# A fused attention and expert kernel: the weighted sum over values as 64x64 native products, the null value subtracted on VectorE, and the norm statistics of the input taken in groups

## Chip, cores and metric

The kernel runs on one core of a Trainium2 chip, as one program. The metric is device microseconds from start to end of an execution.

## What is computed

The input x is 32 sequences of 64 tokens with 256 features. A layer norm, a causal attention of 16 heads that share one key and one value head, a decayed retrieval, a two-of-eight expert layer and a dense layer follow. The change touches the attention, of which this is the core (`nk` and `nv` are a null key and a null value):

```python
xn = ln(x, g_norm)
q = (xn @ Wq).reshape(b, n, HEADS, DIM_HEAD).transpose(0, 2, 1, 3)
kv = xn @ Wkv
k, v = (kv[..., :DIM_HEAD], kv[..., DIM_HEAD:])
k = jnp.concatenate([nk, k], axis=1)
v = jnp.concatenate([nv, v], axis=1)
...
attn = jax.nn.softmax(sim + attn_bias, axis=-1)
out = jnp.einsum('bhij,bjd->bhid', attn, v)
return ln(out @ Wout, g_out)
```

Since the weights of a row sum to 1, the kernel computes the sum over v - nv without the null column and adds nv afterwards.

## The kernel before

**Tiles and steps.** Two sequences make a tile of 128 rows, so there are 16 tiles. Every engine runs a hand-written `body(i, par, live, part)` for i = -2 to 18; `live(off)` says whether tile i + off exists. So in one step an engine works on up to five tiles: tile i + 1 is projected, tile i scored, tile i - 1 weighted and summed, tile i - 2 projected out, tile i - 3 put through the retrieval. Steps -2 to 3 and 14 to 18 are written out, with one-off work between them (`at_step`, and the functions given to `pipeline`); steps 4 to 13 are a loop. There is no scheduler: each engine executes in the order written and waits on semaphores.

**TensorE, step i.** Output projection of tile i - 2 from the upper and lower halves of oT (16 products, lines 322 and 323, then 8, line 1339); transposes of kn2 (1344), of qn (1351, two groups of four), of xn of tile i + 1 (1357); two products of the retrieval (1363, 1369), of which the second waits for qT; scores (1375): 32 products of 64x64 by 65 columns in native float32; 1388; transposes of the weights pr (1400); the qkv projection of tile i + 1 (317 to 319) into banks 3, 2, 1, three split passes for each half of the 256 features, with the null product (1417) at the end of bank 3; transposes of zn (1407); the weighted sum (AV); 317 to 319 for the retrieval's output; 1443.

**Split and native.** Most matrices are held as two float32r halves (`_h`, `_l`), and `split_passes` multiplies three times. For AV, `vblk` is a 128x128 block matrix that carries the value tile twice on its diagonal, in an upper half (copied by ScalarE, 713, four 64x64 pieces) and a lower half (subtracted by VectorE, 986, four pieces). The weights are transposed into PSUM and split too (ScalarE 683, VectorE 1015). AV is then two sequences by three passes of 512 columns. The null value reaches bank 3 by a product of two rows, `ones` by `nvhl` (1417).

**Norms.** For tile i + 2 VectorE takes bn_stats and bn_aggr (974, 978) between the two parts of the q and k norm sums (1020, 1023), and GpSimd makes scale and bias in four small operations (564 to 570), ahead of `mask_bias` (524). ScalarE then makes xn (660).

**VectorE's order, steady step:** vblk_l, statistics of the output norm (974, 978), xnT_l (993), at (998), sim (1004, three), mx (1007), rT_l (1011), pT_l (1015), ss and sc, statistics of x, ss and sc twice, oT_l (1038, two), den (1041), rden (1044), xs (1047), qn (1055, three). **GpSimd's:** pr (542), which needs rden; output norm (545 to 551); every second step the half of an expert's weights (528); sim less its maximum (556); rn (561, three); norm of x; biasm (524). After step -1 GpSimd copies the null key into kh (496), for which TensorE waits before step 0. After the last tile GpSimd scatters the rows to the experts (579), 32 indirect transfers one after the other.

## Time and profile before

| | us |
|---|---|
| timed runs (3) | 531.86, 532.69, 539.52 |
| median | 532.69 |
| profiled execution, span from first to last instruction | 532.0 |
| PE busy | 468.7 (88%) |
| DVE busy | 359.7 (68%) |
| ACT busy | 274.7 (52%) |
| POOL busy | 284.7 (54%) |

The profile gives no other time of the profiled execution than its span, so times of the trace are set against 532.0. PE is TensorE's matmuls, DVE VectorE, ACT ScalarE, POOL GpSimd. A matmul's record is longer than the time until the next can start, since matmuls are pipelined; where they follow without a wait, the distance between starts is the cost. A native float32 product has two records, a split pass and a transpose one.

### The profile page before, as it was taken

What the parts mean: (1) busy time and instruction counts of PE and PEld (TensorE: products, weight loads), DVE (VectorE), ACT (ScalarE), POOL (GpSimd) and SP (SyncE); (2) the same over time, 40 slices, a digit from 0 to 9 for tenths busy, and PEclk for the clock granted to TensorE, in tenths of its full rate; (3) what the DMA queues carried; (4) which work ended last, traced back from release to release, by engine and by line L of the source; (5) the groups of instructions that cost most, each with busy time, mean ns of one, the idle gap of its engine ahead of it and who ended that gap; (6) DMA issues with size and microseconds to landing.
All of it is one profiled execution on the core that took longest, in us unless ns stands there. A gap on an engine that the chain in (4) does not pass through costs nothing.

```text
span 532.0 us, 11898 instructions
## 1 busy us (share of the span) xinstructions
PE 468.7 (88%) x3961; PEld 418.7 (79%) x3961; DVE 359.7 (68%) x879; ACT 274.7 (52%) x574; POOL 284.7 (54%) x343
## 2 busy tenths in 40 slices
PE   3946889999999999999999896499989489999997
PEld 1735777898999988898888785398989359898986
DVE  4784888888889888898766475757664524444522
ACT  3426666576667666566652422246565234453442
POOL 3738778897987979797830777400000633425100
PEclk9966999999999999999998998989999879999999
DMA  8370103709082641000010323265752312213011
GB/s 263 90 192 1 31 1 111 257 26 343 0 292 72 208 157 30 0 30 1 1 31 2 99 100 108 82 206 185 235 169 100 89 33 57 80 41 96 25 41 39
DMA packets 51616, 52.17 MB, mean 98 GB/s; under 512 B 6645, under 2 KB 49015, under 8 KB 51577
## 3 DMA queue, kind: packets, MB, share of 16 engines
q1 hardware_dynamic: 47956, 42.98, 25.5%
q0 software_dynamic: 3072, 8.39, 5.0%
q8 instruction: 23, 0.38, 0.3%
q10 hardware_dynamic: 548, 0.28, 0.2%
q14 instruction: 17, 0.13, 0.1%
HBM read 22.03 MB, written 29.62 MB: 97 GB/s over the span
## 4 chain that ended last, share of the span: by engine, by line
PE 59%; issue 8%; POOL 8%; ACT 5%; DMA 3%; DVE 3%; SPq 1%; DVEq 0%; ACTq 0%; POOLq 0%
PE bank L317 10%; PE bank L318 9%; PE bank L319 9%; POOL slot_x L579 6%; PE bank L322 5%; PE bank L323 5%; PE bank L1375 3%; PE bank L1655 3%; PE bank L1400 2%; PE bank L1339 2%; PE bank L1443 2%; ACT qT L666 2%; PE bank L1351 1%; PE bank L1388 1%; DMA slot_y<-yb 1%
## 5 line engine op out<-in xcount | busy, mean ns | idle before, releaser
L588 POOL DMA_INDIRECT yg<-slot_y,yrow x32 | 34.2, 1068 | 120.8 <-DMA slot_y<-yb 76.3
L561 POOL TENSOR_TENSOR rn<-sc,half 128x6 f32<-128x6 f32 (+1 forms) x48 | 60.6, 1277 | 7.9 <-DVE sc L1023 6.9
L1256 DVE TENSOR_TENSOR hl<-hw,hh 128x512 fp32r<-128x512 f32 x32 | 22.2, 693 | 57.1 <-ACT hw L837 57.1
L835 ACT ACTIVATE hh<-bank,late 128x512 fp32r<-128x512 f32 x32 | 22.0, 688 | 53.5 <-PE bank L1655 41.9
L317 PE MATMUL bank<-wqkv_h,xnT_h 128*128 128x384 f32 x96 | 39.1, 408 | 6.8 <-DVE sim L1004 6.8
L556 POOL TENSOR_TENSOR sim<-sim,mx 128x1040 f32<-128x1040 f32 x16 | 31.3, 1955 | 23.0 <-DVE mx L1007 23.0
L695 ACT ACTIVATE sq<-bank 128x384 f32<-128x384 f32 (+1 forms) x48 | 22.8, 475 | 40.3 <-PE bank L319 24.7
L524 POOL TENSOR_TENSOR biasm<-bias,mneg 128x1040 f32<-128x1040 f32 x16 | 35.7, 2229 | 3.7 <-DMA bias<-rel_scratch 3.7
L579 POOL DMA_INDIRECT slot_x<-xs,posi x32 | 31.4, 980 | 11.2 <-issue 9.4
L542 POOL TENSOR_TENSOR pr<-pe,rden 128x1024 f32<-128x1024 f32 x16 | 30.4, 1903 | 9.2 <-DVE rden L1044 4.5
L322 PE MATMUL bank<-wout_h,oT_h 128*128 128x256 f32 x128 | 33.6, 296 | 1.9 <-DVE oT_l L1038 1.9
L318 PE MATMUL bank<-wqkv_l,xnT_h 128*128 128x384 f32 x96 | 34.5, 359 | 0.0
L319 PE MATMUL bank<-wqkv_h,xnT_l 128*128 128x384 f32 x96 | 34.3, 358 | 0.0
L322 PE MATMUL bank<-w_h,hh 128*128 128x256 f32 x128 | 32.5, 287 | 0.0
L323 PE MATMUL bank<-wout_l,oT_h 128*128 128x256 f32 x128 | 32.4, 289 | 0.0
L323 PE MATMUL bank<-w_l,hh 128*128 128x256 f32 x128 | 32.0, 283 | 0.0
L1020 DVE TENSOR_REDUCE ss<-sq 128x6 f32<-128x384 f32 (+1 forms) x48 | 25.2, 526 | 7.5 <-ACT sq L695 7.4
L1004 DVE TENSOR_TENSOR sim<-bank,biasm 128x455 f32<-128x455 f32 (+1 forms) x48 | 21.9, 513 | 11.2 <-PE bank L1375 11.2
L674 ACT ACTIVATE zn<-bank,nb,rs 128x256 f32<-128x256 f32 x16 | 9.1, 566 | 39.4 <-POOL nb L551 39.4
L317 PE MATMUL bank<-wu_h,bxT_h 128*128 x80 | 25.1, 314 | 2.5 <-DVE bxT_l L1205 2.5
L322 PEld LDWEIGHTS bank<-wout_h,oT_h 128*128 128x128 f32 x128 | 24.9, 195 | 2.5 <-issue 1.4
L317 PEld LDWEIGHTS bank<-wqkv_h,xnT_h 128*128 128x128 f32 x96 | 19.5, 204 | 9.1 <-issue 8.3
(317 smaller groups left out, 1604.8 us busy)
## 6 DMA issues: line engine op xcount, KB each, us to landing
slot_x<-zrow SPq DMA_DIRECT2D x4, 4352.0 KB, 14.4
xq<-slot_x SPq DMA_DIRECT2D x40, 128.0 KB, 2.1
slot_y<-yb SPq DMA_DIRECT2D x20, 256.0 KB, 2.4
fstage<-in_f_W SPq DMA_DIRECT2D x4, 512.0 KB, 4.5
out<-p_all SPq DMA_DIRECT2D x8, 256.0 KB, 2.1
xs<-in_x SPq DMA_DIRECT2D x1, 1536.0 KB, 9.5
raw_out<-in_c_Wout SPq DMA_DIRECT2D x1, 1024.0 KB, 7.8
stage<-in_m_wgate SPq DMA_DIRECT2D x8, 128.0 KB, 2.1
```

Source lines behind the costliest of these rows:

```text
L317: e.matmul(dst, stat[0], mov[0], start=start, stop=False, **kw)
L318: e.matmul(dst, stat[0], mov[1], start=False, stop=False, **kw)
L319: return e.matmul(dst, stat[1], mov[0], start=False, stop=stop, **kw)
L322: e.matmul(dst, stationary, moving[0], start=start, stop=False, **kw)
L323: e.matmul(dst, stationary, moving[1], start=False, stop=False, **kw)
L524: e.tensor_tensor(biasm[:, :, :], bias[:, :, :], (mneg[:, i:i + 1, :] if isinstance(i, int) else mneg[:, bass.ds(i, 1), :]).to_broadcast([ ...
L542: e.tensor_tensor(pr[:, :].rearrange('p (h k) -> p h k', h=H), pe[:, :, 0:S], rden[:, :].rearrange('p (h o) -> p h o', o=1).to_broadcast([ ...
L556: e.tensor_tensor(sim[:, :, :], sim[:, :, :], mx[:, :].rearrange('p (h o) -> p h o', o=1).to_broadcast([P, H, NK]), ALU.subtract).then_inc ...
L561: e.tensor_tensor(rn[:, lo:hi], sc[:, lo:hi], half[:, lo:hi], ALU.pow).then_inc(sems['rn'], 1)
L579: e.indirect_dma_start(out=xdram.ap()[:, :], out_offset=bass.IndirectOffsetOnAxis(ap=posi[:, t, r:r + 1], axis=0), in_=xs[:, t, :], in_off ...
L588: e.indirect_dma_start(out=yg[:, g % 2, r, t, :], out_offset=None, in_=ydram.ap()[:, :], in_offset=bass.IndirectOffsetOnAxis(ap=yrow[:, g ...
L1020: e.reduce_sum(ss[:, lo:hi], sq[:, lo:hi, :], AX_X).then_inc(sems['ss'], 1)
```

## The change

- **AV.** `split_passes` with `vblk` and the halves of pT is replaced by four native float32 products of 64x64 by 512 columns, one for each quarter of the array. For that the head parity of the second sequence is swapped: rows r of qT meet sequence b at r ^ b, in scores and AV, and the biases and null biases are loaded in the same order (three transfers for the bias, not two; two for `nulls`, not one). pT is one float32 copy; pT_l, vblk_h, vblk_l and their zeroing go.
- **Null value.** The product 1417 goes. VectorE makes v_own and v_other (three operations of 64 columns) from bank 3 less `nvB`, at the end of its step.
- **Norm of x.** Statistics of x are taken for groups of tiles, 1, 1, 2, 4, 4 and 4 of them: `row_stats(n)` on VectorE at the start of step -2 and at the very end of steps -1 to 3, `norm_rows(n)` on GpSimd after the same steps. The loop has none of it.
- **Order.** ScalarE makes kn2 before oT_h and exp, not after. VectorE makes qn before xs, den and rden. TensorE's eight lower passes of the output projection come after the transposes of qn, and the waits of AV stand before the last bank of qkv.

```diff
+        X_GROUPS = ((0, 1), (1, 2), (2, 4), (4, 8), (8, 12), (12, NT))
+
+        def x_groups_for(i):
+            return [n for n, (lo, hi) in enumerate(X_GROUPS) if lo <= i < hi][0] + 1 if isinstance(i, int) else len(X_GROUPS)
...
+            def norm_rows(n):
+                t0, t1 = X_GROUPS[n]
+                e.wait_ge(sems['mvx'], 2 * (n + 1))
+                e.tensor_tensor(nmx[:, t0:t1], mvx[:, t0:t1, 0], fixed[:, 1:2].to_broadcast([P, t1 - t0]), ALU.mult)
+                e.tensor_tensor(vex[:, t0:t1], mvx[:, t0:t1, 1], fixed[:, 0:1].to_broadcast([P, t1 - t0]), ALU.add).then_inc(sems['ln1_ve'], 1)
+                e.wait_ge(sems['ln1_ve'], n + 1)
+                e.tensor_tensor(rsx[:, t0:t1], vex[:, t0:t1], half[:, 0:t1 - t0], ALU.pow).then_inc(sems['ln1_rs'], 1)
+                e.wait_ge(sems['ln1_rs'], n + 1)
+                e.tensor_tensor(nbx[:, t0:t1], nmx[:, t0:t1], rsx[:, t0:t1], ALU.mult).then_inc(sems['ln1_nb'], 1)
...
                 e.wait_ge(sems['rn'], NB3)
-                e.wait_ge(sems['ln1_nb'], 2)
+                norm_rows(1)
                 e.wait_ge(sems['v_null'], 2)
                 e.tensor_copy(kh[:, :, S], colsc[:, NKK:NKK + 1].to_broadcast([P, 2])).then_inc(sems['p_tables'], 1)
...
             def after_first_scores():
+                norm_rows(2)
...
             def mask_decay():
+                norm_rows(4)
...
             def after_second_scores():
+                norm_rows(3)
...
-                    e.wait_ge(sems['ln1_nb'], due(i + 2 if live(1) else NT))
...
-                    e.wait_ge(sems['mv1'], due(2 * (i + 3)))
...
-                    e.tensor_tensor(nb1[:, :], nm1[:, :], rs1[:, :], ALU.mult).then_inc(sems['ln1_nb'], 1)
...
+            pipeline(e, body, {-2: after_norm0, -1: after_first_projection, 0: after_first_scores, 1: after_second_scores, 2: mask_decay, 3: lambda: norm_rows(5)})
...
+                    e.wait_ge(sems['ln1_nb'], x_groups_for(i + 1 if isinstance(i, int) else i))
...
+                    e.activation(xn[:, :], at_tile(xs, i + 1), ACT.Identity, bias=at_col(nbx, i + 1), scale=at_col(rsx, i + 1)).then_inc(sems['xn'], 1)
...
+                        e.activation(pT[:, 4 * c:4 * c + 4, :], bank[4 + c][:, :].rearrange('p (b t) -> p b t', b=4), ACT.Copy).then_inc(sems['pT'], 1)
...
+                if live(1):
+                    e.wait_ge(sems['rn'], due(NB3 * (i + 1) + 1))
+                    e.wait_ge(sems['kT_t'], due(i + 1))
+                    e.activation(kn2[:, :, :], bank[NB3][:, QB - 2 * DH:QB - DH].rearrange('p (o d) -> p o d', o=1).to_broadcast([P, 2, DH]), ACT.Copy, scale=rn[:, H:H + 1]).then_inc(sems['kn2'], 1)
...
-                if live(1):
-                    e.wait_ge(sems['av_t'], due(2 * i))
-                    e.wait_ge(sems['qkv'], due(NB3 * (i + 2)))
-                    for b, r in ((0, 0), (0, 1), (1, 0), (1, 1)):
-                        last = e.activation(vblk_h[r * DH:(r + 1) * DH, 1 - par, b, r * DH:(r + 1) * DH], bank[NB3][b * S:(b + 1) * S, QB - DH:QB], ACT.Copy)
-                    last.then_inc(sems['v_h'], 1)
-                    e.wait_ge(sems['rn'], due(NB3 * (i + 1) + 1))
-                    e.wait_ge(sems['kT_t'], due(i + 1))
-                    e.activation(kn2[:, :, :], bank[NB3][:, QB - 2 * DH:QB - DH].rearrange('p (o d) -> p o d', o=1).to_broadcast([P, 2, DH]), ACT.Copy, scale=rn[:, H:H + 1]).then_inc(sems['kn2'], 1)
...
+            def row_stats(n):
+                t0, t1 = X_GROUPS[n]
+                e.wait_ge(sems[('ld_x0', 'ld_x0', 'ld_x1', 'ld_x2', 'ld_x2', 'ld_x2')[n]], 16 * 1)
+                for t in range(t0, t1):
+                    last = e.bn_stats(stx[:, t - t0, :], xs[:, t, :])
+                last.then_inc(sems['mvx'], 1)
+                e.wait_ge(sems['mvx'], 2 * n + 1)
                 settle(e)
-                e.bn_aggr(mv[:, n, :], st6[:, n, :]).then_inc(sems[m], 1)
+                for t in range(t0, t1):
+                    last = e.bn_aggr(mvx[:, t, :], stx[:, t - t0, :])
+                last.then_inc(sems['mvx'], 1)
+                e.wait_ge(sems['mvx'], 2 * n + 2)
 
...
+                if isinstance(i, int) and i == FIRST_I:
+                    row_stats(0)
...
-                if live(0):
...
-                        last = e.tensor_tensor(vblk_l[at_b], bank[NB3][b * S:(b + 1) * S, QB - DH:QB], vblk_h[at_b].bitcast(F32), ALU.subtract)
...
-                if live(-1):
-                    for c in range(2):
-                        e.wait_ge(sems['pT_h'], due(2 * (i - 1) + c + 1))
-                        e.tensor_tensor(pT_l[:, 4 * c:4 * c + 4, :], bank[4 + c][:, :].rearrange('p (b t) -> p b t', b=4), pT_h[:, 4 * c:4 * c + 4, :].bitcast(F32), ALU.subtract).then_inc(sems['pT_l'], 1)
...
-                if live(2):
-                    if isinstance(i, int):
-                        e.wait_ge(sems['ld_x0' if i + 2 < 2 else 'ld_x1' if i + 2 < 4 else 'ld_x2'], 16 * 1)
-                    layer_norm_stats(at_tile(xs, i + 2), 0, i + 2, 'mv1', 'ln1_nb')
...
-                if live(0):
-                    e.wait_ge(sems['pe'], due(i + 1))
-                    e.reduce_sum(den[:, :], pe[:, :, :], AX_X).then_inc(sems['den'], 1)
-                    e.wait_ge(sems['den'], due(i + 1))
-                    e.wait_ge(sems['pr'], due(i))
-                    e.reciprocal(rden[:, :], den[:, :]).then_inc(sems['rden'], 1)
-                if live(-3):
-                    e.wait_ge(sems['vo_t'], due(i - 2))
-                    e.tensor_tensor(at_tile(xs, i - 3), bank[4][:, 0:D], at_tile(xs, i - 3), ALU.add).then_inc(sems['x1'], 1)
...
+                if live(-3):
+                    e.wait_ge(sems['vo_t'], due(i - 2))
+                    e.tensor_tensor(at_tile(xs, i - 3), bank[4][:, 0:D], at_tile(xs, i - 3), ALU.add).then_inc(sems['x1'], 1)
+                if live(0):
+                    e.wait_ge(sems['pe'], due(i + 1))
+                    e.reduce_sum(den[:, :], pe[:, :, :], AX_X).then_inc(sems['den'], 1)
+                    e.wait_ge(sems['den'], due(i + 1))
+                    e.wait_ge(sems['pr'], due(i))
+                    e.reciprocal(rden[:, :], den[:, :]).then_inc(sems['rden'], 1)
+                if live(1):
+                    e.wait_ge(sems['av_t'], due(2 * i))
+                    if isinstance(i, int) and i == -1:
+                        e.wait_ge(sems['v_nv'], 1)
+                    values = slice(QB - DH, QB)
+                    e.tensor_tensor(v_own[:, 1 - par, :], bank[NB3][:, values], nvB[:, :], ALU.subtract)
+                    for b in range(2):
+                        other = slice((1 - b) * S, (2 - b) * S)
+                        last = e.tensor_tensor(v_other[other, 1 - par, :], bank[NB3][b * S:(b + 1) * S, values], nvB[b * S:(b + 1) * S, :], ALU.subtract)
+                    last.then_inc(sems['v'], 1)
+                if isinstance(i, int) and FIRST_I < i < FIRST_I + len(X_GROUPS):
+                    row_stats(i - FIRST_I)
...
                     for c in range(HP):
                         upper_passes(e, bank[6][:, 0:D], (wout_h[:, c, :], wout_l[:, c, :]), oT_h[:, c, :], c == 0)
-                    e.wait_ge(sems['oT_l'], due(2 * (i - 1)))
-                    for c in range(HP):
-                        last = e.matmul(bank[6][:, 0:D], oT_l[:, c, :], wout_h[:, c, :], start=False, stop=c == HP - 1)
...
-                    e.wait_ge(sems['x1'], due(i - 3))
...
+                if live(-2):
+                    e.wait_ge(sems['oT_l'], due(2 * (i - 1)))
+                    for c in range(HP):
+                        last = e.matmul(bank[6][:, 0:D], oT_l[:, c, :], wout_h[:, c, :], start=False, stop=c == HP - 1)
+                    last.then_inc(sems['wo_t'], 1)
...
+                    e.wait_ge(sems['v'], due(i + 1))
...
-                    head = slice(r * DH, (r + 1) * DH)
                     for b in range(2):
+                        head = slice((r ^ b) * DH, ((r ^ b) + 1) * DH)
                         last = e.matmul(dst[b * S:(b + 1) * S, lo:lo + NK], qT[head, c, b * S:(b + 1) * S], kh[head, b, :], start=True, stop=True)
...
+                def before_av():
+                    e.wait_ge(sems['pT'], due(2 * i))
+                    e.wait_ge(sems['v'], due(i))
+                    e.wait_ge(sems['zn'], due(i - 1))
+                    e.wait_ge(sems['rT_l'], due(i - 2))
...
+                        if m == NB3 - 1 and live(-1):
+                            before_av()
...
-                        if c == NB3 - 1:
-                            last = e.matmul(bank[NB3][:, QB - DH:QB], ones[0:2, :], nvhl[:, :], start=False, stop=True, skip_group_check=True)
...
-                    e.wait_ge(sems['pT_l'], due(2 * i))
-                    e.wait_ge(sems['vblk'], due(i))
-                    e.wait_ge(sems['zn'], due(i - 1))
-                    e.wait_ge(sems['rT_l'], due(i - 2))
-                    for b in range(2):
-                        last = split_passes(e, bank[6 + b][:, :], (vblk_h[:, 1 - par, b, :], vblk_l[:, 1 - par, b, :]), (pT_h[:, :, b * S:(b + 1) * S], pT_l[:, :, b * S:(b + 1) * S]), True, True)
-                        last.then_inc(sems['av_t'], 1)
+                    if not live(1):
+                        before_av()
+                    for q in range(2):
+                        rows = slice(q * S, (q + 1) * S)
+                        for b in range(2):
+                            r = q ^ b
+                            value = (v_other if r else v_own)[rows, 1 - par, :]
+                            last = e.matmul(bank[6 + b][r * DH:(r + 1) * DH, :], value, pT[rows, :, b * S:(b + 1) * S], start=True, stop=True)
+                            if q == 1:
+                                last.then_inc(sems['av_t'], 1)
```

What VectorE does between the norm of q of one step and the scores of the next, steps 1 and 2 of the kernel before:

```order
L1038 SCALAR_TENSOR_TENSOR oT_l<-bank,colsc,oT_h 128x8x64 x2
L1041 TENSOR_REDUCE den<-pe 128x16
L1044 RECIPROCAL rden<-den 128x16
L1055 TENSOR_TENSOR qn<-bank,rn 128x256
L1055 TENSOR_TENSOR qn<-bank,rn 128x384 x2
L986 TENSOR_TENSOR vblk_l<-bank,vblk_h 64x64 x4
L974 BN_STATS st<-bank 128x6
L254 MEMSET carrier 128x1
L978 BN_AGGR mv<-st 128x2
L993 TENSOR_TENSOR xnT_l<-bank,xnT_h 128x256
```

and the same place now, with the statistics of tiles 4 to 7 (stx, mvx) in it:

```order
L1030 SCALAR_TENSOR_TENSOR oT_l<-bank,colsc,oT_h 128x8x64 x2
L1038 TENSOR_TENSOR qn<-bank,rn 128x256
L1038 TENSOR_TENSOR qn<-bank,rn 128x384 x2
L1044 TENSOR_REDUCE den<-pe 128x16
L1047 RECIPROCAL rden<-den 128x16
L1053 TENSOR_TENSOR v_own<-bank,nvB 128x64
L1056 TENSOR_TENSOR v_other<-bank,nvB 64x64 x2
L972 BN_STATS stx<-xs 128x6 x4
L253 MEMSET carrier 128x1
L977 BN_AGGR mvx<-stx 128x2 x4
L987 BN_STATS st<-bank 128x6
```

The three qn moved ahead of den and rden, and four bn_stats and four bn_aggr stand between the value pieces and the next step's work.

GpSimd, after step 1, before:

```order
L561 TENSOR_TENSOR rn<-sc,half 128x6 x2
L564 TENSOR_TENSOR nm<-mv,fixed 128x1
L565 TENSOR_TENSOR ve<-mv,fixed 128x1
L568 TENSOR_TENSOR rs<-ve,half 128x1
L570 TENSOR_TENSOR nb<-nm,rs 128x1
L524 TENSOR_TENSOR biasm<-bias,mneg 128x1040
L542 TENSOR_TENSOR pr<-pe,rden 128x1024
```

and now:

```order
L581 TENSOR_TENSOR rn<-sc,half 128x6 x2
L545 TENSOR_TENSOR biasm<-bias,mneg 128x1040
L494 TENSOR_TENSOR nmx<-mvx,fixed 128x4
L495 TENSOR_TENSOR vex<-mvx,fixed 128x4
L497 TENSOR_TENSOR rsx<-vex,half 128x4
L499 TENSOR_TENSOR nbx<-nmx,rsx 128x4
L562 TENSOR_TENSOR pr<-pe,rden 128x1024
```

The norm of x moved from ahead of biasm to between biasm and pr, and it waits for the statistics that VectorE makes last in the step.

## Rows read from the trace of the kernel before

**Rows 1.** Busy time by stretch: window, its length, busy us and count of each engine, clock.
```profile
105.21:254.33 149.12, 146.29 (x1561) 134.19 (x1561) 131.59 (x328) 98.80 (x225) 127.93 (x146) 1.00 0.31 103
```

**Rows 2.** Timeline of PE, one steady step: start, us, line, operands, count, idle before.
```profile
149.91 0.39 PE L317 MATMUL bank<-pT_h,vblk_h 128*128 128x512 f32 x1
...
151.30 0.28 PE L317 MATMUL bank<-wvo_h,rT_h 128*128 128x256 f32 x1
...
152.03 1.06 PE L1443 MATMUL bank<-znT,mqk 128*128 128x128 f32 x8
...
157.68 0.49 PE L1369 MATMUL bank<-uT,znT 128*128 128x128 f32 x2 [0.27 <-ACT qT L666]
158.10 1.15 PE L1375 MATMUL bank<-kh,qT 64*64 64x65 f32 x60
159.18 0.71 PE L1388 MATMUL bank<-at,zn 128*128 128x128 f32 x4
...
161.90 0.33 PE L319 MATMUL bank<-wqkv_h,xnT_l 128*128 128x384 f32 x1
162.16 0.29 PE L1417 MATMUL bank<-nvhl,ones 2*128 2x64 f32 x1
...
162.66 0.34 PE L318 MATMUL bank<-wqkv_l,xnT_h 128*128 128x384 f32 x1
```

**Rows 3.** Timeline of DVE, the same step.
```profile
151.59 1.41 DVE L1038 SCALAR_TENSOR_TENSOR oT_l<-bank,colsc,oT_h 128x512 fp32r<-128x512 f32 x2 [0.20 <-ACT oT_h L704]
...
154.91 1.34 DVE L1055 TENSOR_TENSOR qn<-bank,rn 128x256 f32<-128x256 f32 x3
156.17 0.91 DVE L986 TENSOR_TENSOR vblk_l<-bank,vblk_h 64x64 fp32r<-64x64 f32 x4
```

**Rows 4.** Groups by line and form, 105.21 to 254.33: busy us, mean ns.
```profile
L568 POOL TENSOR_TENSOR rs<-ve,half 128x1 f32<-128x1 f32 x10 | 5.5, 548 | 0.8
...
L974 DVE BATCH_NORM_STATS2 st<-xs 128x6 f32 x9 | 3.8, 427 | 0.0
...
L978 DVE BATCH_NORM_AGGREGATE mv<-st 128x2 f32<-128x6 f32 x19 | 3.4, 180 | 0.5
```

**Rows 5.** Timeline of PE, start of the kernel.
```profile
27.91 0.33 PE L1344 MATMUL bank<-ident,kn 128*128 128x128 f32 x1 [1.28 <-POOL kh L496]
...
37.71 0.66 PE L317 MATMUL bank<-wqkv_h,xnT_h 128*128 128x384 f32 x1 [5.76 <-DVE sim L1004]
...
55.64 0.42 PE L317 MATMUL bank<-wqkv_h,xnT_h 128*128 128x384 f32 x1 [0.54 <-DVE sim L1004]
```

**Rows 6.** The page's clock row: granted TensorE clock in 40 slices, tenths of full speed.
```profile
PEclk9966999999999999999998998989999879999999
```

**Rows 7.** Timeline of DVE, step 2.
```profile
62.55 1.24 DVE L1041 TENSOR_REDUCE den<-pe 128x16 f32<-128x1040 f32 x1 [0.18 <-ACT pe L708]
```

**Rows 8.** Timeline of POOL, step 2.
```profile
66.40 1.90 POOL L542 TENSOR_TENSOR pr<-pe,rden 128x1024 f32<-128x1024 f32 x1 [0.31 <-issue]
```

**Rows 9.** Timeline of PE, AV and the transposes of pr, steps 2 to 4.
```profile
59.28 0.39 PE L317 MATMUL bank<-pT_h,vblk_h 128*128 128x512 f32 x1
...
68.36 1.09 PE L1400 MATMUL bank<-ident,pr 128*128 128x128 f32 x8
...
73.81 0.39 PE L317 MATMUL bank<-pT_h,vblk_h 128*128 128x512 f32 x1
...
85.59 1.09 PE L1400 MATMUL bank<-ident,pr 128*128 128x128 f32 x8
...
90.33 0.39 PE L317 MATMUL bank<-pT_h,vblk_h 128*128 128x512 f32 x1
...
100.48 1.09 PE L1400 MATMUL bank<-ident,pr 128*128 128x128 f32 x8
```

**Rows 10.** Timeline of PE, AV after the last projection.
```profile
268.05 0.50 PE L317 MATMUL bank<-pT_h,vblk_h 128*128 128x512 f32 x1 [0.24 <-DVE pT_l L1015]
```

**Rows 11.** Timeline of POOL, the first scatter to the experts.
```profile
296.15 1.25 POOL L579 DMA_INDIRECT slot_x<-xs,posi  x1 [1.71 <-DVE posi L1118]
```

More of the change, by code:

```diff
@@ L131, in adaln_attention_ffn @@
             kh = s1('kh', [P, 2, NK])
-            vblk_h = s1('vblk_h', [P, 2, 2, P], F32R)
-            vblk_l = s1('vblk_l', [P, 2, 2, P], F32R)
+            v_own = s1('v_own', [P, 2, DH])
+            v_other = s1('v_other', [P, 2, DH])
             sim = s1('sim', [P, H, NK])
@@ L233, in adaln_attention_ffn @@
                     t_hT t_mlp t_fold    unit_h unit
-                    mv1 ln1_ve ln1_rs ln1_nb xn xnT xnT_h xnT_l qkv sq ss ss_c rn qn kn2 v_h
-                    kT_t kh sc7 vblk qT_t qT sim_t biasm sim mx simc pe den rden pr
-                    pT_t pT_h pT_l av_t oT_h oT_l wo_t mv2 ln2_ve ln2_rs ln2_nb zn
+                    mvx ln1_ve ln1_rs ln1_nb xn xnT xnT_h xnT_l qkv sq ss ss_c rn qn kn2 v
+                    kT_t kh sc7 qT_t qT sim_t biasm sim mx simc pe den rden pr
+                    pT_t pT av_t oT_h oT_l wo_t mv2 ln2_ve ln2_rs ln2_nb zn
                     znT_t znT uT_t uT sc_t at rt_t rT_h rT_l vo_t x1
```

93 lines of the change are left out of this document (34 added, 59 removed).

## The prediction

> **What bounds the kernel now.** I read first the busy time by stretch. From the AV of step 4 to that of step 14, 105.21 to 254.33, PE is busy for 146.29 of 149.12 us at a granted clock of 1.00 [rows 1]. That is ten steps of 14.91 us and PE bound. DVE is next with 131.59 of 149.12, so a shorter PE step soon meets DVE. Then I read the timelines of one such step on PE and DVE, for distances between starts [rows 2, 3]. What is saved there reaches the end one for one, because the 32 scatters that follow the pipeline start only when the router's positions are there [rows 11], and nothing behind them is touched. Last I read steps -1 to 4. There PE is no bound: it waits for kh, sim and pr [rows 5, 9], and the change puts work on exactly these chains. So the sum has two halves, a steady gain and a cost at the edge.
>
> **The steady step.** *AV.* Six split passes take 151.30 - 149.91 = 1.39 us, 0.23 each [rows 2]. Now it is four native products of 512 columns, eight records. Eight native records of 128 columns take about 1 us (L1443, 1.06 with the last one's tail), so 128 columns cost some 0.12 and 512 some 0.45. Whether the quarters work at once decides: 60 score records of 64x65 take 159.18 - 158.10 = 1.08 us, 18 ns each, although one lasts far longer, so there four quarters do run abreast [rows 2]. I take two passes, all quarters abreast, 0.9, and 0.3 for entering and leaving the 64x64 form: 1.2, a gain of 0.2. Bounds are 0.9 and 3.6 (all eight in turn).
>
> *Null product.* From 161.90 to 162.66 two starts lie 0.76 apart where two passes of 384 columns would take 0.34 (0.17 each, three quarters of the 0.23 of 512); L1417 costs 0.42, and it goes [rows 2].
>
> *qT wait.* L1369 waits 0.27 for qT, and its records end in 158.10 - 157.68 = 0.42 where four of 0.12 stand for two products [rows 2]; the eight lower passes, some 1 us (256 columns each, 0.12), now stand between the transposes of qn and this product. I take 0.45 of stall and 0.1 of refill off, -0.5, if DVE gives qn no later. DVE's qn starts at 154.91, 5.0 behind AV [rows 3]; with den, rden and xs behind it, it starts at 3.4. The v pieces are new: three of 64 columns, at the 0.23 of one of the four vblk_l (0.91) [rows 3], 0.7 against 0.91. pT_l, vblk_l and bn_stats with bn_aggr of x (0.43 and 0.18) leave DVE [rows 4]; with pT_l of 1024 columns at the rate of oT_l (1.41 for as many, rows 3) and the lighter v its load falls by some 2.1 us a step. ACT loses four small copies, GpSimd 1.2 us (one power of 0.55 and three small operations, rows 4). In the other direction, AV and kn2 wait for work later on ACT's and GpSimd's orders every second step, about 0.1.
>
> Sum: -0.2 - 0.4 - 0.5 + 0.1 = -1.0 us a step, bounds -0.7 and -1.1, so 13.9 instead of 14.9. Over ten steps -10.
>
> **The edges.** Here each item delays a chain on which PE waits.
>
> (a) Step -1. kT_0 at 27.91 waited 1.28 for kh on GpSimd [rows 5]. `norm_rows(1)` (1.3 us) needs `row_stats(1)`, which DVE now takes after qn (three, 1.3) and v (0.7), where it stood ahead of the second sums. I work it out as +2.6, plus 0.3 for the further transfer of nulls: +2.9 on 27.91, and so on 37.71. Bounds +1.5 and +3.5.
>
> (b) Step 0, QKV of tile 1. The null product goes, -0.45 at that clock. The clock row shows 0.6 in two slices of 13.3 us, 26.6 to 53.2 [rows 6]; if it comes back at the same moment as before, a part of the 6 us of passes runs at 2.4 and not at 1.2 GHz: -1.2 (0 to -1.7). xn of tile 2 in step 1 then waits for the group of tiles 2 and 3, whose statistics follow rden and v, and for GpSimd's norm behind biasm: +2.5. Altogether QKV of tile 2 (55.64 [rows 5]) at +3.7, and less its null product +3.3.
>
> (c) Step 2. Now DVE's den starts at 62.55 [rows 7]. With qn ahead (1.3) it starts at 63.7, rden ends at 65.2, v at 65.9. Four bn_stats at 0.43 and four bn_aggr at 0.18 [rows 4] with a settle make 2.6: 68.5. GpSimd has been waiting in `norm_rows(3)`; its four operations, of four columns, take 1.3 to 1.7: 70.1. Behind them stands pr, which started at 66.40 and lasts 1.90 [rows 8]: ends 72.1. PE's transposes of pr stood at 68.36, 9.1 behind AV [rows 9]; they slip by 3.7. QKV of tile 3 stood 0.5 later than it had to, by sim, so 3.2 of it remain, less 0.4 of the null product: +2.8.
>
> (d) Step 3, the same group size with the decay mask in front. The transposes stood at 85.59, 11.8 behind AV [rows 9], so much of it was there already; I work out pr's end at 13.4 behind AV: +1.25 net.
>
> (e) Step 4. The transposes stood at 100.48, 10.2 behind AV [rows 9]. GpSimd has the weight split in this step and is late by 0.7; pr's end comes at 14.0: +3.5 net.
>
> Sum of the edges: 3.3 + 2.8 + 1.25 + 3.5 = +10.9, bounds +7 and +14 (they differ by the settle and waits between engines that these chains take seven times, and by the clock).
>
> **The tail.** Step 15 saves the qT wait (0.5), AV 14 stood at 268.05 waiting 0.24 for pT_l, which is gone [rows 10], and steps 14 to 15 save AV: -1.5. The scatters, 296.15 on, each some 1.25 us [rows 11], are as before.
>
> Total: -10 + 10.9 - 1.5 = -0.6 on the span of 532.0, 531.4. The median of the runs shown lies 0.7 above this span, so 532.0 in its terms. Two of a hundred, which is about what a measurement tells from no change, are 522.0 and 543.3.
>
> **Rivals.**
>
> 1. *The edges are cheap.* The grouped statistics hide behind waits that I have put on the path, above all in step -1 and step 4, or PE catches up in steps 5 and 6, since DVE and GpSimd now have slack there. For it: PE's waits for sim (5.76 at 37.71, [rows 5]) show slack of other engines in steps 0 and 1. Against it: at 68.36 the transposes start within 0.1 of pr's end [rows 8, 9], so there a delay goes straight to PE. Half of the edge cost gone is 526, the lowest bound (+4, and the steady step at -1.1) some 521. Range 519 to 526.
>
> 2. *The clock falls.* In steps 2 to 4 PE would stand still for up to 4 us at a time, and the granted clock was low at the start, in a stretch where PE waited 5.76 us [rows 5, 6]. If it falls once, I take 5 us of columns at half the clock, less what the waits hide: +4, so 536.
>
> 3. *The quarters do not run abreast where two row halves write to one bank; slower.* Before, the row halves of the scores wrote different banks (bank 2 - r) at all but the last pair, so the 18 ns a record say nothing of one bank. Now both row halves of AV write bank 6 + b, and by r ^ b those of the scores one bank too, with other partitions. If they take turns there, AV has four passes of 0.45 in place of two, +0.9 a step over 16 steps: +14, 546. With the scores, whose 1.08 would then be 2.0, it is 560. It decides from +0.7 a step, where ten steps give 2%. For it, that nothing in this trace shows the overlap on one bank; against it, that the last pair (bank 3, both halves) does so within 60 records at no visible cost.
>
> The Trainium skill says in TensorEngine Tiling (Array Packing), "Gotcha 1: PSUM Pressure", that different row tiles cannot access the same PSUM bank simultaneously. By that rule the third rival would be the outcome, 546 to 560; no stretch of this trace shows it for long operands, and the last pair speaks against it for short ones.
>
> 4. *All eight records in turn*, 3.6 for AV: +35, 567. The 18 ns speak against it.
>
> **How the numbers follow.** Forecast 0.56 (526 to 538 as its own range); cheap edges 0.24; clock 0.10; one bank 0.08; in turn 0.02. The likeliest gives 532.0. The range goes from 522.5, within the first rival, to 543, past the second; left out are about 0.11 below and 0.10 above. Faster by over 2%: half of the first rival, 0.12. Slower: the last two, 0.10. Within 2%: 0.78.
>
> **What would show it.** Steady distance between AVs 13.9; AV itself 1.2, with eight records, and vo right behind; L1369's wait gone. kT_0 at about 30.8. In steps 2, 3 and 4 PE waits some 3.5, 1.5 and 3.5 us at the transposes of pr, released by GpSimd, and GpSimd's wait ahead of it ends on mvx of DVE. Scatters begin at 295.5. It is wrong in the edges if PE's wait in step 4 is under 2 us; wrong in AV if the eight records take over 1.6; wrong in the steady step if PE waits at oT_l or at `at` for 0.3 or more.

## The result, and the profile after

| | before | changed |
|---|---|---|
| timed runs | 531.46, 531.86, 532.69, 539.52 | 535.91, 536.45, 541.78, 544.53 |
| median, us | 532.28 | 539.12 |
| span of the profiled execution | 532.0 | 534.1 |

The ratio is 1.0103, 95% interval 1.0058 to 1.0147: 1% slower, within 2%, and inside the range of 522.5 to 543. The two executions over 1.5% above the fastest of their kernel, 539.52 and 544.53, count in the medians but not in the ratio. The forecast was 532.0 and no change, so it missed by a loss that is clear of noise. The profiled execution of the changed kernel is its fastest, 535.91. It is 2.1 us longer than the one before, and this is what the traces account for; the rest of the median's 6.8 us these two traces do not show; I come to it under e8 and e12.

The page of the changed kernel:

```profile
span 534.1 us, 11692 instructions
...
PE 464.9 (87%) x3977; PEld 408.3 (76%) x3977; DVE 337.3 (63%) x816; ACT 261.3 (49%) x510; POOL 275.4 (52%) x302
...
PEclk9956889979999999999998998979999969999999
```

Every engine has less to do, DVE by 22 us. The clock row has about what [rows 6] had at the third and fourth slice (5 and 6, where it was 6 and 6), and new falls at the fifth, sixth and ninth (53 to 80 and 107 to 120 us).

Busy time by stretch, the same view as [rows 1]; the last column but two is the granted clock. First the stretch without PE work in step 2 and the 4 us behind it, then a stretch behind a shorter wait in step 3, then the wait of step 4 and the 4 us behind it, last the ten steady steps:

```profile
69.30:73.20 3.90, 0.00 (x0) 0.00 (x0) 3.79 (x12) 0.00 (x0) 3.47 (x6) 1.00 0.02 4
73.20:77.20 4.00, 3.94 (x17) 3.94 (x18) 0.56 (x4) 1.91 (x4) 2.92 (x6) 0.57 0.00 0
90.40:94.40 4.00, 3.58 (x18) 3.20 (x19) 2.86 (x5) 0.82 (x3) 3.79 (x6) 0.57 0.00 0
104.50:109.50 5.00, 0.01 (x1) 0.02 (x1) 2.47 (x13) 0.99 (x3) 2.53 (x5) 0.84 1.04 346
109.50:113.50 4.00, 3.99 (x68) 3.56 (x69) 1.25 (x3) 1.74 (x4) 1.98 (x5) 0.50 0.40 134
119.05:258.62 139.57, 139.57 (x1571) 124.09 (x1570) 116.19 (x271) 90.77 (x185) 117.09 (x106) 1.00 0.33 110
```

Ten steps take 139.57 in place of 149.12, 13.96 each. Timeline of PE in one of them, answering to [rows 2]:

```profile
160.97 0.64 PE L1441 MATMUL bank<-pT,v_own 64*64 64x512 f32 x1
160.98 0.65 PE L1441 MATMUL bank<-pT,v_other 64*64 64x512 f32 x2
160.99 1.05 PE L1441 MATMUL bank<-pT,v_own 64*64 64x512 f32 x2
161.46 0.60 PE L1441 MATMUL bank<-pT,v_other 64*64 64x512 f32 x2
161.47 0.59 PE L1441 MATMUL bank<-pT,v_own 64*64 64x512 f32 x1
161.99 0.39 PE L323 MATMUL bank<-wvo_h,rT_h 128*128 128x256 f32 x1
...
168.12 0.48 PE L1373 MATMUL bank<-uT,znT 128*128 128x128 f32 x2
168.53 1.15 PE L1379 MATMUL bank<-kh,qT 64*64 64x65 f32 x60
169.61 0.71 PE L1392 MATMUL bank<-at,zn 128*128 128x128 f32 x4
```

The eight records of AV start in two groups, 0.01 us apart within a group and 0.49 from one group to the next: four quarters work at once, with both row halves on one bank. AV takes 161.99 - 160.97 = 1.02 us (1.39 before). The scores, now with both row halves on one bank too, still take 1.08. L1373 waits for nothing.

The edge, PE's timeline with its waits (from kT of step 0 to the AV of step 4), answering to [rows 5] and [rows 9]:

```profile
29.55 0.48 PE L1342 MATMUL bank<-ident,kn 128*128 128x128 f32 x1 [3.62 <-POOL kh L514]
...
38.61 0.66 PE L323 MATMUL bank<-wqkv_h,xnT_h 128*128 128x384 f32 x1 [4.09 <-DVE sim L1005]
...
60.80 0.64 PE L1441 MATMUL bank<-pT,v_own 64*64 64x512 f32 x1
...
73.26 1.55 PE L1404 MATMUL bank<-ident,pr 128*128 128x128 f32 x8 [4.01 <-POOL pr L562]
...
79.26 0.64 PE L1441 MATMUL bank<-pT,v_own 64*64 64x512 f32 x1
...
90.79 1.17 PE L1392 MATMUL bank<-at,zn 128*128 128x128 f32 x4 [1.60 <-DVE at L999]
...
97.68 0.64 PE L1441 MATMUL bank<-pT,v_own 64*64 64x512 f32 x1
...
109.51 0.66 PE L1361 MATMUL bank<-ident,xn 128*128 128x128 f32 x2 [4.99 <-ACT kh L673]
...
119.05 0.64 PE L1441 MATMUL bank<-pT,v_own 64*64 64x512 f32 x1
```

The AV of steps 1 to 4, which is that of tiles 0 to 3, begins at 60.80, 79.26, 97.68 and 119.05, in place of 59.28, 73.81, 90.33 [rows 9] and 105.21 [rows 1]; the distances are the prediction's steps 2, 3 and 4. (The expectations below call the last of them the AV of step 3, after its tile.) The loss is 1.5 before the first of these, then 3.9, 1.9 and 6.5, together 13.8 us (13.84). The steady steps give 9.55 of it back, the last two steps 1.15, the way from there to the end 1.0: +2.1.

### The profile page after: what moved, and what is told of

The parts are those of the page before. It is cut to its first block, busy times and chain, and to the rows that moved or that the text cites. A ratio compares the mean times of both kernels' runs of the same rounds, so it can differ in the third digit from the quotient of the medians.

```text
span 534.1 us, 11692 instructions
## 1 busy us (share of the span) xinstructions
PE 464.9 (87%) x3977; PEld 408.3 (76%) x3977; DVE 337.3 (63%) x816; ACT 261.3 (49%) x510; POOL 275.4 (52%) x302
## 4 chain that ended last, share of the span: by engine, by line
PE 64%; POOL 10%; issue 9%; DVE 8%; ACT 4%; DMA 3%; SPq 1%; DVEq 0%; ACTq 0%; POOLq 0%
PE bank L323 9%; PE bank L324 8%; PE bank L325 8%; POOL slot_x L590 6%; PE bank L328 5%; PE bank L329 5%; PE bank L1379 4%; PE bank L1404 3%; PE bank L1667 3%; PE bank L1441 3%; PE bank L1350 2%; PE bank L1355 2%; PE bank L1455 2%; PE bank L1392 2%; POOL yg L599 1%
## 5 line engine op out<-in xcount | busy, mean ns | idle before, releaser
L1260 DVE TENSOR_TENSOR hl<-hw,hh 128x512 fp32r<-128x512 f32 x32 | 22.2, 693 | 57.8 <-ACT hw L842 57.8
L705 ACT ACTIVATE sq<-bank 128x384 f32<-128x384 f32 (+1 forms) x48 | 22.8, 475 | 30.8 <-PE bank L325 30.4
L1030 DVE SCALAR_TENSOR_TENSOR oT_l<-bank,colsc,oT_h 128x512 fp32r<-128x512 f32 x32 | 22.5, 746 | 12.4 <-ACT oT_h L718 12.4
```

## Experiments

Each ran with a profile and, beside it, the kernel before on the same chip. The kernel before took 547.0 beside e1 to e4, 532.6 beside e5 to e8, and 546.7 beside e9 to e12, so only ratios compare the totals of different groups; inside a trace I use the step length, the AV starts, and the first scatter, which ends the part that the change touches.

### e1 and e11: the statistics per tile again

```diff
-                if isinstance(i, int) and FIRST_I < i < FIRST_I + len(X_GROUPS):
-                    row_stats(i - FIRST_I)
...
                     sums(0)
+                if live(2):
...
+                    layer_norm_stats(at_tile(xs, i + 2), 0, i + 2, 'mv1', 'ln1_nb')
```

(and GpSimd's four operations of one column back ahead of biasm.)

> The changed kernel with one part undone: the statistics of x and the norm's scale and bias are made per tile again, in their old places on VectorE (between the two parts of the sums) and GpSimd (ahead of biasm); AV, null value and order stay new. Theory 1 (the 13.8 us lost up to the AV of step 3 are the grouped statistics, standing in front of pr, xn and at): the AV of step 3 comes at 104 to 107 us in place of 119.05, no wait of PE for pr or xn in steps 2 and 4, the granted clock stays full after 60 us, the step stays at 13.96, and the time is 519 to 523. Theory 2 (it is the new order, with qn ahead of den and kn2 ahead of exp, that makes pr late, and the group adds little): the AV of step 3 stays behind 112 and the time over 528. Rival within theory 1: 0.6 us more on VectorE and 1.2 on GpSimd a step make the steady step 14.3, then 524 to 526.

Measured: ratio 0.9758 (0.9716 to 0.9800). Run again in another group (e11):

> e1_ungroup once more, beside e9_best and e12_before on one chip: the steps 13.94 and 14.36 again, the first scatter 13 to 15 us before that of e12_before. In e1_ungroup the way from the first scatter to the end was 248.9 us, against 235.8 in the profile of the kernel before, taken on another chip; if that belongs to the chip or the execution and not to the kernel, here it is the same as in e12_before within 1 us, or the runs of one kernel spread by 5 to 10 us.

Ratio 0.9765 (0.9735 to 0.9795). In e1 the transposes of pr in step 4 start at 95.8, in place of 100.5 before and 114.6 in the changed kernel, and the AV behind them at 100.2, earlier than either theory had it. The clock does not fall there, and the steady step is 14.17, not 13.96, so that the rival within theory 1 (14.3) was nearer; here the two stretches of the edge and the steady steps:

```profile
57.00:85.00 28.00, 23.43 (x279) 20.59 (x276) 23.77 (x54) 19.65 (x39) 24.42 (x30) 1.00 0.04 10
85.00:113.00 28.00, 27.51 (x314) 24.26 (x312) 23.65 (x62) 17.04 (x37) 24.44 (x30) 1.00 0.51 167
95.82:237.47 141.65, 140.12 (x1575) 123.82 (x1571) 120.22 (x301) 87.83 (x185) 127.89 (x146) 1.00 0.35 115
```

So theory 1 holds: without the grouping the rest of the change is 2.4% faster than the kernel before, and this version beats both. The AV of step 4 comes 18.8 us earlier than in the changed kernel (17.6 in e11, at 101.4), more than the 13.8 of the loss: without the grouping the rest of the change shortens the edge too, by 1.5 us beside the kernel before on the same chip (e12, 102.9). e11's first scatter, at 285.0, comes 8.9 before that of e12 at 293.9, not 13 to 15: the expectation had set e1 against a trace of another chip. e1 pays 0.2 us a step in the steady state: 13.9 and 14.4 by turns, the latter where GpSimd also splits an expert's weights, so that rn, and behind it kn2, oT_h and oT_l, come late. That is what the grouping had bought in the ten steady steps, 2 us.

### e2: the grouping alone

```diff
+                if isinstance(i, int) and FIRST_I < i < FIRST_I + len(X_GROUPS):
+                    row_stats(i - FIRST_I)
...
+            pipeline(e, body, {-2: after_norm0, -1: after_first_projection, 0: after_first_scores, 1: after_second_scores, 2: mask_decay, 3: lambda: norm_rows(5)})
```

> The kernel before with only the grouping of the statistics put in (VectorE takes them after qn at the end of steps -1 to 3, GpSimd at its new places); products, value blocks and order are the old ones. Theory 1: the steady step stays 14.9 (PE bound), the edge costs 9 to 14 us, so 541 to 546. Theory 2: the grouping alone costs under 5 us, so under 538.

Ratio 1.0288 (1.0245 to 1.0331), +15.7 us on a kernel before of 547; the steady step stays 14.91. pr's transposes of step 4 start at 113.5 in place of 100.5, and the AV behind them at 118.3 in place of 105.2, 13 us later. Theory 1 again, from the other side.

### e3 and e7: the order without the products, the products without the order

e3 is e1 with the old order:

```diff
-                if live(-2):
-                    e.wait_ge(sems['oT_l'], due(2 * (i - 1)))
-                    for c in range(HP):
-                        last = e.matmul(bank[6][:, 0:D], oT_l[:, c, :], wout_h[:, c, :], start=False, stop=c == HP - 1)
-                    last.then_inc(sems['wo_t'], 1)
...
```

(these lines back ahead of the transpose of kn2, kn2 behind exp on ScalarE, den, rden and xs ahead of qn on VectorE.)

> As e1_ungroup, and the order is the old one too: kn2 after exp, den, rden and xs before qn, the lower passes of the output projection before the transposes. What stays of the change is the native AV on values less the null value and the dropped null product. From distances in the trace (AV 1.39 to 1.02, the last bank 0.3 less, 0.1 for entering AV, the qT wait back) the step should be 14.3 to 14.4, and the time 524 to 527. If the order gives nothing it equals e1_ungroup within 1 us; if the order is what costs at the edge it is faster than e1_ungroup.

Ratio 0.9911 (0.9879 to 0.9942). The step is 14.78, not 14.3 to 14.4: a miss. With the old order PE's transposes of qn start 0.42 behind that of kn2 where they start 0.11 behind it in the changed kernel (and in the kernel before, where PE came later), and the wait for qT is there again:

```profile
167.24 0.27 PE L1335 MATMUL bank<-ident,kn 128*128 128x128 f32 x1
167.66 1.12 PE L1343 MATMUL bank<-ident,qn 128*128 128x128 f32 x8
...
169.49 0.49 PE L1361 MATMUL bank<-uT,znT 128*128 128x128 f32 x2 [0.27 <-ACT qT L670]
```

So PE's shorter products are mostly eaten by waits on the chain through kn2, qn and qT; products and null value alone are worth 0.13 us a step.

e7 is the other half, the kernel before with PE's lower passes moved and qn ahead of xs, den and rden, kn2 left where it was:

```diff
+                        if c == 0:
+                            e.wait_ge(sems['x1'], due(i - 3))
...
+                if live(-2):
+                    e.wait_ge(sems['oT_l'], due(2 * (i - 1)))
```

> The kernel before with a part of the new order alone: PE's lower passes of the output projection behind the transposes of qn, and on VectorE qn ahead of xs, den and rden; kn2 stays where it was on ScalarE, behind exp and the value blocks, products, value blocks and statistics are the old ones. If the wait for qT (0.44) is an item of its own, the step falls from 14.91 to 14.4 to 14.5 and the time by 7 to 8 us (ratio 0.986). If the order pays only with the shorter products and the lighter ScalarE, since qn still waits for kn2, the step stays over 14.7 (ratio 0.994 or more).

Ratio 1.0264 (1.0231 to 1.0298). The step is 16.0: over 14.7, as the second theory had it, but neither theory had foreseen a loss. VectorE stands before qn, and PE before its second product of the retrieval; timeline of both in one step:

```profile
157.56 1.35 DVE L1046 TENSOR_TENSOR qn<-bank,rn 128x256 f32<-128x256 f32 x3 [1.36 <-ACT kn L717]
...
162.12 0.48 PE L1371 MATMUL bank<-uT,znT 128*128 128x128 f32 x2 [0.70 <-DVE vblk_l L986]
```

kn2 is still behind exp and the four copies of vblk_h on ScalarE, so qn, now first on VectorE, holds up den, rden and vblk_l behind it. So this part of the order costs by itself. Whether the old products with kn2 first as well would gain was not tried.

### e4: PE kept busy where it stood still

```diff
+                if isinstance(i, int) and i == 2:
+                    for _ in range(32):
+                        e.transpose(bank[4][:, 0:P], ident[:, :], ident[:, :])
```

(and 12 of them in step 3 ahead of the wait for at; the results are overwritten, so these products only keep PE at work.)

> The changed kernel with 32 idle transposes of the identity on PE in step 2 ahead of the transposes of pr (where PE stood still for 4.0 us) and 12 in step 3 ahead of the second product of the retrieval (1.6 us). They take about 3.5 and 1.3 us and shift nothing if they end in the wait. Theory A (the granted clock falls to half because PE stood still there): the clock is 1.00 between 73 and 77 us and at 91, where it was half, and up to 2 us are gained before step 4; the fall after the 5 us stall of step 4 stays. Theory B (the clock falls whatever PE does there): the same dips, and the time is the same or 1 us more.

Busy time by stretch, behind the filled wait of step 2, and at the wait of step 4, which wasn't filled:

```profile
72.00:76.00 4.00, 3.83 (x26) 3.79 (x27) 1.33 (x7) 2.44 (x6) 3.03 (x6) 1.00 0.00 0
...
105.00:110.00 5.00, 3.17 (x62) 2.89 (x64) 0.72 (x2) 2.73 (x6) 3.41 (x7) 0.52 0.69 235
```

Theory A: the clock stays full in steps 2 and 3, and falls in step 4 as before. From the transposes of pr in step 2 to those in step 3 it is 17.57 us in place of 19.15 (92.41 - 73.26); 1.6 us of that distance were the clock. Against e8, a second execution of the changed kernel in which the distance is 20.24, it is 2.7. Ratio 1.0027 (1.0005 to 1.0050); the changed kernel wasn't run on that chip.

### e6: ScalarE's wait in the loop

```diff
-            return [n for n, (lo, hi) in enumerate(X_GROUPS) if lo <= i < hi][0] + 1 if isinstance(i, int) else len(X_GROUPS)
+            return [n for n, (lo, hi) in enumerate(X_GROUPS) if lo <= i < hi][0] + 1 if isinstance(i, int) else 4
```

> The changed kernel with one number changed: in the loop ScalarE waits for four groups of norms (tiles 0 to 7) ahead of xn, not for all six, so that in step 4 it no longer waits for the norm of tiles 12 to 15, which GpSimd makes at the very end of the edge. [...] Theory of the trace of the changed kernel (only xn's wait and the clock after it): the same wait gone and hardly a wait left, step 4 under 16, over 5 us faster.

The rival to this is the prediction's own theory: in step 4 it is pr that comes late, behind the norm of the last group, and that wait stays when xn's is gone. With the edit the loop no longer waits for the last two groups at all, so the edit is good for measuring only.

In the changed kernel, before this edit, the timeline of the engines other than PE at the end of step 4's wait reads:

```profile
104.61 1.40 DVE L972 BATCH_NORM_STATS2 stx<-xs 128x6 f32<-128x256 f32 x4
...
106.15 0.28 DVE L977 BATCH_NORM_AGGREGATE mvx<-stx 128x2 f32<-128x6 f32 x3
...
108.04 0.20 POOL L499 TENSOR_TENSOR nbx<-nmx,rsx 128x4 f32<-128x4 f32 x1
...
108.50 0.60 ACT L670 ACTIVATE xn<-xs,nbx,rsx 128x256 f32 x1 [7.13 <-POOL nbx L499]
```

ScalarE had been free for 7.1 us; behind xn stand kh and qT, for which PE waits. With the edit, PE in step 4:

```profile
109.89 0.68 PE L1392 MATMUL bank<-at,zn 128*128 128x128 f32 x4 [1.64 <-DVE at L999]
...
112.55 1.06 PE L1404 MATMUL bank<-ident,pr 128*128 128x128 f32 x8 [1.72 <-POOL pr L562]
```

The step from pr to pr is 18.3 us (112.55 - 94.28) in place of 22.2, and from AV to AV 18.25 (116.94 - 98.69) in place of 21.37; a step under 16 did not come. So the prediction's mechanism was there, hidden behind the wait for xn. Now pr is what comes late, 13.9 us behind AV (98.69), and PE's standstill is in two pieces of 1.6 and 1.7. The stretch with these waits and the one behind it:

```profile
108.00:112.00 4.00, 1.20 (x24) 0.83 (x14) 3.63 (x14) 0.00 (x0) 3.16 (x5) 1.00 1.04 347
112.00:116.00 4.00, 3.45 (x24) 3.44 (x25) 1.01 (x3) 2.31 (x6) 3.22 (x6) 1.00 0.23 79
```

The clock stays at 1.00. Ratio 1.0082 (1.0029 to 1.0135), where e8, the changed kernel on the same chip, has 1.0214.

### e5, e9, e10: better places for the statistics

e5 takes them for two tiles in every second step, e10 moves them to VectorE's wait for the scores and GpSimd's wait for the maximum, e9 also gives the weight split to VectorE.

```diff
-                if live(2):
+                if live(2) and par == 0:
```

> As e1_ungroup, but the statistics of x are taken for two tiles at a time in the even steps (two bn_stats, two bn_aggr, one set of four small operations of two columns) and not at all in the odd steps, where GpSimd has the split of an expert's weights. In e1_ungroup even steps are 13.94 and odd ones 14.36, with PE waiting in the odd ones for oT_l behind GpSimd's late subtraction. If GpSimd's 1.2 us in the odd steps are the cause, both become 13.96 to 14.0 and the kernel is 1.5 to 2.5 us faster than e1_ungroup; if it is VectorE's 0.6 us or nothing of the two, the odd steps stay at 14.3. Edges as in e1_ungroup (within 1 us). Ratio to before 0.971 to 0.973.

> From e1_ungroup (changed kernel, statistics of x per tile), two moves. VectorE takes the statistics of x between the product at and the scores' sim, where it waited 0.5 us for PE, and GpSimd makes scale and bias ahead of its subtraction of the maximum, where it waited 0.9. And the split of an expert's weights goes from GpSimd to VectorE, ahead of the sums (768 columns, about 0.9 us, in a wait of 0.75 to 0.9). In e1_ungroup the odd steps were 14.4 because rn, and behind it kn2 and oT_h, came late by GpSimd's 1.85 us split. If that is the cause, both steps are 13.94 to 14.0, and the first scatter comes 2 us earlier than in e11_ungroup, 14 to 17 us earlier than in the kernel before. If VectorE has become the bound instead, steps are 14.1 to 14.4 and nothing is gained.

```diff
-                    split_unit(part[0])
...
+                    e.tensor_tensor(at_tile(wu_l, u), stage[:, :], at_tile(wu_h, u).bitcast(F32), ALU.subtract).then_inc(sems['unit'], 1)
```

> As e9_best, but the split of the expert's weights stays on GpSimd: only the statistics and norm of x are moved out of the way of the sums and rn. If it is the split that makes rn late in the odd steps, they stay at 14.2 to 14.4, 1 to 2 us slower than e9_best at the first scatter; if it is the statistics between the sums, both steps are at 13.96 here too.

All three missed. e5: steps of 14.1 and 14.65, ratio 0.9907 (0.9888 to 0.9926). In its timeline GpSimd works from the rn of a step with statistics through norm, biasm, pr, output norm, split and maximum to the rn of the next with no wait over 0.41 us, so the statistics had been put into the same stretch as the split. e10: 13.9 and 15.0, ratio 0.9818 (0.9789 to 0.9846). There GpSimd waits 0.95 for rden ahead of pr and not at all from pr through the moved norm of x (1.2 us) and the split to rn: the norm left a place with room for one without. Neither reading was tested further. e9: 13.9 and 15.2, ratio 0.9876 (0.9832 to 0.9920), its first scatter 3.4 us behind e11's instead of 2 before. The split on VectorE, in e9, in a steady step:

```profile
169.99 1.93 POOL L568 TENSOR_TENSOR sim<-sim,mx 128x1040 f32<-128x1040 f32 x1 [0.64 <-DVE mx L996]
170.16 2.58 DVE L1004 TENSOR_TENSOR wu_l<-stage,wu_h 128x768 f32 x1
...
175.61 1.41 DVE L1022 SCALAR_TENSOR_TENSOR oT_l<-bank,colsc,oT_h 128x512 fp32r<-128x512 f32 x2 [0.90 <-ACT oT_h L710]
```

I had put it at 0.9 us and it took 2.58. The same subtraction in step 1 of e9, started just ahead of GpSimd's, and after the last tile, with GpSimd idle:

```profile
51.67 0.95 DVE L1004 TENSOR_TENSOR wu_l<-stage,wu_h 128x768 fp32r<-128x768 f32 x1
51.83 2.58 POOL L568 TENSOR_TENSOR sim<-sim,mx 128x1040 f32<-128x1040 f32 x1 [1.99 <-DVE mx L996]
...
285.41 0.95 DVE L1004 TENSOR_TENSOR wu_l<-stage,wu_h 128x768 fp32r<-128x768 f32 x1
```

So alone it costs what I had put. Where it starts 0.17 behind GpSimd's subtraction of the maximum it lasts until 0.8 after the end of that one; where it starts first, it is GpSimd's that takes 2.58 and not 1.93. Of e5, e9 and e10 none beats e1.

### e8 and e12: the two kernels again

> The changed kernel itself once more, beside the others on one chip: AV of step 3 at 119 us, steady step 13.96, the clock at half after the standstills of steps 2 and 4 (about 74 to 77, 107 to 113 us), ratio to before 1.005 to 1.012.

Ratio 1.0214 (1.0183 to 1.0245) beside the same kernel before as e5 to e7: the ratio missed, by a loss twice the first one. The steady steps are as they were (13.96). The AV of step 4 is at 120.66 and not 119.05, and the share of each step in the edge shifts by up to 1.3 us. In step 3 PE waits 1.60 for at, as in the first profile, and then 0.66 for pr, and the clock stays full where it was at 0.57:

```profile
91.99 0.68 PE L1392 MATMUL bank<-at,zn 128*128 128x128 f32 x4 [1.60 <-DVE at L999]
...
90.40:94.40 4.00, 1.74 (x15) 1.52 (x16) 2.75 (x5) 0.00 (x0) 3.66 (x8) 1.00 0.00 0
```

The first scatter is at 300.5 (298.9 in the first profile of it), but from there to the end it is 242.0 us, not 235.2: the granted clock is at half from about 308 to 321 us, and PE's products for the router's second batch, which the second half of the scatters waits for, take longer:

```profile
306.00:310.00 4.00, 4.00 (x24) 3.58 (x22) 1.75 (x3) 0.92 (x2) 3.08 (x4) 0.74 0.32 111
310.00:320.00 10.00, 10.00 (x32) 8.09 (x32) 4.30 (x35) 1.48 (x3) 7.56 (x9) 0.50 0.29 102
```

> The kernel before itself, with a profile, beside the others on one chip: steps of 14.91, the first scatter at 296 us. Its way from there to the end tells what of the differences there belongs to the execution.

Ratio to itself 0.9987 (0.9971 to 1.0003). The steps are 14.9 and the first scatter is at 293.9, 2.3 us before that of the first profile, all of it lost or won before the AV of step 1. From the first scatter to the end e12 takes 251.0 us and e11, on the same chip, 250.8, where the first profile of the kernel before took 235.8. On this chip VectorE waits long for the router's logits, and GpSimd's scatters stop in their middle. Timelines of e12, then of e11:

```profile
316.85 0.29 DVE L1082 TENSOR_REDUCE lg<-bank 128x64 f32<-128x128 f32 x1 [7.10 <-remote]
...
324.69 0.96 POOL L579 DMA_INDIRECT slot_x<-xs,posi  x1 [10.56 <-DVE posi L1118]
```

```profile
307.93 0.29 DVE L1074 TENSOR_REDUCE lg<-bank 128x64 f32<-128x128 f32 x1 [7.10 <-remote]
```

In the first profile of the kernel before that same wait of VectorE was 1.48, and no scatter waited. So 6.8 us of this part (changed kernel) and 15.2 (kernel before) belong to the execution or the chip, not to the change. How much of the 6.8 us between the first medians is such a fall, more frequent by chance or because of the change, stays open: two of the four first runs of the changed kernel (541.78 and 544.53) have a mean clock of 0.927 and 0.931, as the four runs of e8 have (0.924 to 0.931), the other two 0.942 and 0.946, as the four of e6 on e8's chip (0.933 to 0.942).

## Why the prediction was wrong

**The steady step was right.** It forecast 13.9 and the step is 13.96. Of its terms AV gave 0.37 instead of 0.2, with 0.09 given back in the passes behind it; the projection up to AV is 0.31 shorter (0.4 forecast), since AV now starts 0.27 behind the last pass where two passes lie 0.17 apart. No run has the 0.3 for entering and leaving the 64x64 form by itself; these two differences, 0.1 each, are all that the rows show of it. The wait for qT went, and 0.42 with it (0.5 forecast). What e3 and e7 add is that these are no separate items: the products alone give 0.13 a step, a part of the order alone costs 1.1, and all of the change together gives 0.95.

**The third and fourth rivals** fell. Both row halves of the array write one bank in AV and in the scores, and four quarters run abreast all the same. By the rule of the Trainium skill that the prediction quoted (TensorEngine Tiling (Array Packing), "Gotcha 1: PSUM Pressure") AV would have cost about 2 and the scores 2.0; they took 1.02 and 1.08. The measurement decides; here the halves write other partitions of the bank, and nothing in these runs shows two row tiles on the same partitions. One argument against the third rival was a wrong reading: of the last pair only one row half is among the 60 records. The other half follows behind the products with at (the kernel scores it last), so the trace before had no overlap on one bank at all.

**The edge is where it failed**: +13.8 us for a forecast of +10.9, and with it the sign of the sum: -9.55 + 13.84 - 1.15 - 1.0 is +2.1 on the span, where -0.6 was forecast. The step that failed is (e), what PE waits for in step 4, and beside it the slow clock behind the waits, which the sum left out. By steps:

- (a) and (b), forecast +3.3 to the AV of tile 0, measured +1.5. kT_0 is at 29.55 and not 30.8. GpSimd's norm stood where I had put it, and PE waits 3.62 for kh in place of 1.28, but its next wait, for sim, is 4.09 in place of 5.76 and left 0.9 of the delay at 38.61. The QKV of tile 2 then stands at 57.46, +1.8 for a forecast of +3.7.
- (c), forecast +2.8, measured +3.9. The mechanism is as told: pr ends 12.4 behind AV, after the norm of four tiles, and PE waits 4.0. What is missing is the clock, at 0.57 over the 4 us behind the wait; e4 gives 1.6 for it up to the transposes of pr in step 3.
- (d), forecast +1.25, measured +1.9. PE waited for at (1.60): the statistics stand ahead of at as well, on VectorE, and GpSimd's norm ahead of the decay mask that at needs. In the first profile the slow clock behind it hid the wait for pr; in e8, at full clock, PE waits 0.66 for pr too, and the step is 17.56 and not 18.42, +1.0.
- (e), forecast +3.5, measured +6.5. Here a step of the argument was wrong: "GpSimd has the weight split in this step and is late by 0.7; pr's end comes at 14.0". The loop's body asks for all six groups ahead of xn, and step 4 is its first pass, so xn waits for the norm of tiles 12 to 15 (108.50, after 7.13), kh and qT stand behind it on ScalarE, and PE stands still for 5 us, at the transposes of xn and not at those of pr; then the clock is at half for 4. That `x_groups_for` gives the full count for a register stood in the diff. With that wait relaxed (e6) pr comes 13.9 behind AV, as forecast, the clock stays full, and the step from AV to AV is 18.25, 3.4 above that of the kernel before: the +3.5 of the forecast. So 3.1 us of (e) are the wait that I had not seen and the clock behind it.

The second rival, the fall of the clock, was put as something that comes in place of the forecast, with 0.10. It came with it: the standstills of 4 and 5 us in the edge are each followed by a stretch at half the clock (1.2 GHz). The one of 1.6 us in step 3 is too in the first profile of the changed kernel, while in e8, the same kernel, and in e6, with the same wait in steps 3 and 4, the clock stays full. Its 5 us of columns came from no row; the rows show 0.57 and 0.50 over some 4 us each. A forecast of long waits on PE should have had this in its sum.

**The first scatter** was forecast at 295.5 and is at 298.9, and at 300.5 in e8. So of e8's loss, 10.8 us by the medians, what lies ahead of the first scatter accounts for some 4.3 (set against the first profile of the kernel before); the rest lies behind it, and how much of that is due to the change stays open, as told above.

**The tail**, forecast -1.5, measured -1.15. **The profiled time** against the median: 532.0 of span were set against a median of 532.7; in every later run the time is 1.7 to 2.2 above the span of the same execution, so the 531.4 of the forecast stood for about 533.2.

**The first rival** (cheap edges) was wrong in its sign for steps 2 to 4, and right for step -1 and 0. Its lowest time was summed wrongly: -11 + 4 - 1.5 is -8.5, which gives 524 and not 521. And 0.7 a step over ten steps is 7 us or 1.3%; it takes the 16 steps to reach 2%. Neither slip touches the forecast.

## What to carry to other kernels

Work that is taken out of a loop of 10 steps and put at the pipeline's start pays only if the start has the room: here a loop that could hide it for 0.2 us a step had it taken away, and the first steps, where TensorE waits for every other engine, paid 13 us in the kernel before (e2) and 18 in the changed one (e1, e11). A one-off block at the end of a step stands ahead of the first instructions of the next step on its own engine, and a loop that waits for "all groups" waits for the last of them in its first pass. Where a forecast has TensorE stand still as long as here (4 and 5 us), put the slow clock behind it into the sum, and compare versions at the last point that the change touches, not at the end, when what follows spreads by more than the change.

## What was not expected of the hardware

- Four native float32 products of 64x64 by 512 columns, two records each, take 1.02 us from the first start to that of the next product, 0.49 from the first group of four to the second, with two row halves on one bank at a time.
- The clock behind a standstill: 3.9 us without PE work were followed by 0.57 over the next 4 us, 5 us by 0.50 over the next 4; with PE fed 32 idle transposes (3.7 us) it stayed 1.00. A wait of 1.60 was followed by 0.57 in one execution of the changed kernel and by 1.00 in another. A standstill isn't the only thing that it fell behind: in e8 it fell at about 308 us, in a stretch in which PE was busy for 4.00 of 4 us.
- A subtraction of 768 columns that GpSimd does in 1.85 us takes 0.95 on VectorE while GpSimd is idle, and 2.58 where it starts just behind one of GpSimd's; where it starts just ahead, GpSimd's takes 2.58 in place of 1.93 (e9).
- The part behind the first scatter took 235.8 us in one execution of the kernel before and 251.0 in another on another chip, with VectorE waiting 7.10 us for something that the profile only calls remote.
